# The shared feed-forward in float32r parts, with its weights in a ring of column pairs and its down products turned round

## The reference

```python
gate = jax.nn.silu(jnp.einsum('ech,ehi->eci', xg, rg))
up = jnp.einsum('ech,ehi->eci', xg, ru)
eout = jnp.einsum('eci,eih->ech', gate * up, rd)
...
routed = jnp.zeros_like(xf).at[dispatch.reshape(-1)].add(contrib.reshape(-1, h))
shared = jax.nn.silu(x @ sg) * (x @ su) @ sd
return shared + SCALE * routed.reshape(b, s, h)
```

## Time and profile before

| | |
|---|---|
| median of 3 runs | 1663.79 us (1660.51 to 1671.43) |
| profiled execution, its own time | 1664.96 us |
| its span | 1663.2 us |
| TensorE busy | 1557.2 us (94%) |
| VectorE, ScalarE, GpSimd busy | 870.3, 734.2, 696.3 us |

### The profile page before, as it was taken

One profiled execution on the slowest core, in us unless ns is written; L12 is line 12 of the kernel. 1 busy time (PEld: TensorE's weight loads), 2 busy tenths in 40 slices (PEclk: granted clock), 3 DMA queues, 4 the chain that ended last, 5 costly groups with the idle time before them and its releaser, 6 DMA issues. The chain is left out here.

```text
span 1663.2 us, 20499 instructions
## 1 busy us (share of the span) xinstructions
PE 1557.2 (94%) x7136; PEld 747.0 (45%) x7136; DVE 870.3 (52%) x2297; ACT 734.2 (44%) x998; POOL 696.3 (42%) x516
## 2 busy tenths in 40 slices
PE   5699999989999999898999898999999999999998
PEld 3423333323333333332333233555656577777755
DVE  7578878888677865556765723343422111111141
ACT  4754666765566655475545466233211111111111
POOL 4437999987799998153210121400000200000070
PEclk9659999999999999999998888999999999999999
DMA  3551033233231320344432015100040005243071
GB/s 96 145 154 32 23 83 74 74 93 78 65 84 33 78 46 14 73 118 108 124 74 64 28 34 166 61 0 0 0 152 4 23 0 184 92 157 119 16 129 23
DMA packets 76178, 121.39 MB, mean 73 GB/s; under 512 B 15192, under 2 KB 53537, under 8 KB 73003
## 3 DMA queue, kind: packets, MB, share of 16 engines
q1 hardware_dynamic: 72155, 113.62, 24.5%
q0 software_dynamic: 3072, 6.03, 2.1%
q10 hardware_dynamic: 848, 0.43, 0.1%
HBM read 85.05 MB, written 36.96 MB: 73 GB/s over the span
## 5 line engine op out<-in xcount | busy, mean ns | idle before, releaser
L1145 POOL TENSOR_TENSOR sb_prob<-sb_prob,sb_weight 128x1024 f32<-128x1024 f32 x192 | 448.4, 2371 | 44.6 <-ACT sb_prob L1361 44.1
L1361 ACT ACTIVATE sb_prob<-wide 128x1024 f32<-128x1024 f32 (+3 forms) x384 | 347.1, 916 | 210.7 <-PE wide L1974 107.4
L1969 PE MATMUL wide<-sb_stack_q,sb_stack_k 99*128 99x512 bf16 (+3 forms) x896 | 285.7, 369 | 17.4 <-ACT sb_prob L1361 7.5
L1656 DVE CUSTOM_DVE_ANT_0 sb_junk<-bank,sb_bias 128x512 bf16<-128x512 f32 x339 | 226.7, 687 | 61.4 <-PE bank L1944 56.3
L1405 ACT ACTIVATE sb_sil<-wide 128x320 f32<-128x320 f32 (+1 forms) x128 | 66.2, 517 | 436.0 <-PE wide L2048 436.0
L1944 PE MATMUL bank<-sb_stack_k,sb_stack_q 96*128 96x512 bf16 (+3 forms) x597 | 217.6, 383 | 20.0 <-DVE sb_rowmax L1656 5.4
L2048 PE MATMUL wide<-sb_weight,sb_ffn 128*128 128x512 f32 x512 | 233.2, 599 | 0.0
L1989 PE MATMUL wide<-sb_prob,sb_v_aug 128*17 128x512 f32 (+3 forms) x1792 | 225.3, 569 | 7.7 <-ACT sb_o_raw L1374 6.0
L1783 DVE TENSOR_TENSOR sb_act_s<-sb_sil,wide 128x512 f32<-128x512 f32 x64 | 43.9, 687 | 255.0 <-ACT sb_sil L1405 255.0
L1183 POOL DMA_INDIRECT sb_weight<-slots_out,sb_slot_r x32 | 31.5, 986 | 283.9 <-issue 282.1
L2048 PE MATMUL wide<-sb_xgT,sb_big 128*128 128x320 f32 x512 | 147.0, 433 | 1.4 <-ACT sb_xgT L1420 1.4
(11 more groups left out here) (272 smaller groups left out, 1827.9 us busy)
## 6 DMA issues: line engine op xcount, KB each, us to landing
sb_stack_k<-parts SPq DMA_DIRECT2D x32, 256.0 KB, 6.8
o_raw<-sb_o_raw SPq DMA_DIRECT2D x32, 256.0 KB, 2.3
sb_big<-rg SPq DMA_DIRECT2D x8, 1024.0 KB, 4.9
sb_big<-ru SPq DMA_DIRECT2D x8, 1024.0 KB, 7.3
sb_big<-rd SPq DMA_DIRECT2D x8, 1024.0 KB, 10.6
sb_stack_q<-parts SPq DMA_DIRECT2D x16, 384.0 KB, 5.1
parts<-sb_o_norm SPq DMA_DIRECT2D x40, 128.0 KB
sb_stack_q<-parts SPq DMA_DIRECT2D x16, 256.0 KB, 5.6
```

The costliest lines, as they stand in the source:

```text
L1145: e.tensor_tensor(p, p, weight_of(*u[1:]), ALU.mult).then_inc(weigh_p.handle, 1)
L1361: e.activation(p[:, :, first:HALF], sc[:, :, first:HALF], ACT.Exp).then_inc(SC.empty_sem(u), 1)
L1656: e.tensor_tensor_reduce(out=junk[:, i % 2, 0:hi - lo], in0=BK.tile(u)[:, 0:hi - lo], in1=bias[:, qt, lo:hi], scale=1.0, scalar=-3e38, op0 ...
L1969: i = e.matmul(sc[:, j * HALF + first:(j + 1) * HALF], stack_k[0:ROWS_M, n % 3, g, kt * P:(kt + 1) * P], stack_q[0:ROWS_M, n % 3, g, half ...
```

## The change

The shared feed-forward is computed from parts. ScalarE copies the weights of a pair of columns (1536 elements a partition), and the tokens of a chunk, to float32r (the high part); GpSimd or VectorE subtracts that from the original (the low part). Gate and up are three products each of high by high, high by low and low by high, with float32r operands. The activation is split in the same way ("act"), and the down products are turned round: weights are the stationary side, 512 tokens the moving one, so the accumulator holds features as rows; VectorE adds it to xT ("total_T") and TensorE transposes the sum back ("yT").

All weights, shared and expert, now come through a ring of five buffers by pairs of columns ("wload", three transfers of 256 KB), the shared ones anew for each chunk. High and low parts have three buffers each. Pairs of chunks 0 and 1, and the first three of chunk 3, get their low part from GpSimd, the others from VectorE. The downs come two columns behind their gate and up (LAG). The sends are spread over steps. An expert's products stay true float32. New and changed functions, cut:

```diff
...
 COLUMNS_S, COLUMNS_R = I_S // P, I_R // P
 CHUNKS = T // HALF
 TPC = HALF // P
+COLUMNS = [("s", tc, i) for tc in range(CHUNKS - 1) for i in range(COLUMNS_S)]
+COLUMNS += [("e", x, i) for x in range(E) for i in range(COLUMNS_R)]
+COLUMNS += [("s", CHUNKS - 1, i) for i in range(COLUMNS_S)]
+N_PAIRS, EARLY, AHEAD_SPLIT = len(COLUMNS) // 2, 2, 3
+RAWS, HIS = 5, 3
...
+def low_by_pool(p):
+    return column_pair(p)[0][1] < CHUNKS // 2 or p in LAST_CHUNK[:AHEAD_SPLIT]
...
+def sends(b):
+    return [("send", b, t) for t in range(b * NT, (b + 1) * NT)]
...
+def columns_of_chunk(plan, kind, x, others, late):
+    n = COLUMNS_S if kind == "s" else COLUMNS_R
+    for i in range(n):
+        k = COLUMNS.index((kind, x, i))
+        plan.append(("gu", kind, x, i))
+        if kind == "s":
+            plan.append(("act", kind, x, i))
+        p = k // 2 + 1
+        if k % 2 == 0 and p in SPLITS and p not in LAST_CHUNK[:AHEAD_SPLIT]:
+            plan += halved(p)
+        if k >= LAG:
+            ended(plan, k - LAG)
+        plan += late.pop(i, [])
         for _ in range(STEPS_PER_COLUMN):
             if others:
                 plan += flat([others.pop(0)])
-    return plan + [("resT", tc), ("down", "s", tc, COLUMNS_S - 1)]
+def halved(p):
+    return [("split", p)] + ([("wload", p + RAWS)] if p + RAWS < N_PAIRS else [])
+def ended(plan, k):
+    of_, x, i = COLUMNS[k]
+    plan.append(("down", of_, x, i))
+    if k % 2 and of_ == "e" and k // 2 + RAWS < N_PAIRS:
+        plan.append(("wload", k // 2 + RAWS))
+    if of_ == "s" and i == COLUMNS_S - 1:
+        plan.append(("total_T", x))
+    if of_ == "e" and i == COLUMNS_R - 1:
+        plan.append(("eout", x))
+def turned(tc):
+    return {LAG + 1: [("yT", tc, 0), ("yT", tc, 1)]}
+FIRST = [("hsplit", 0), ("split", 0)]
...
     last, route = (1, 1, NQ // 2 - 1), route_plan(0)
...
+    others = [("num", *last), *route[:3], ("inv", *last), *route[3:5], ("times", *last), PAUSE]
+    mixer = mix_plan(1)
+    at = mixer.index(("hT", 1, 0, DC - 1))
+    mixer = mixer[:at + 1] + [("hsplit", 2)] + mixer[at + 1:]
+    others += beside(sends(0), [outputs(1, 1)[k:k + NH] for k in (0, NH)] + mixer)
+    plan = [("wload", RAWS)]
+    columns_of_chunk(plan, "s", 0, others, {COLUMNS_S - 4: [("hsplit", 1)]})
+    columns_of_chunk(plan, "s", 1, others, turned(0))
+    plan += flat(others) + [("pad",)]
+    columns_of_chunk(plan, "s", 2, route_plan(1) + sends(1), turned(1))
+    plan.append(("fetch", 0))
     for x in range(E):
...
+        late = turned(2) if x == 0 else {}
+        if x + 1 < E:
+            late[3] = late.get(3, []) + [("fetch", x + 1)]
+        if x == 2:
+            late[4] = [("hsplit", 3)]
+        if x == E - 1:
+            for k in range(AHEAD_SPLIT):
+                late[2 * k + 3] = late.get(2 * k + 3, []) + halved(LAST_CHUNK[k])
+        columns_of_chunk(plan, "e", x, [], late)
     last = B * NT - TPC
...
+    others = [PAUSE] * 4 + [("gather", t) for t in range(AHEAD)] + [PAUSE] * 2
     for t in range(B * NT):
         others += [[("combine", t), ("gather", t + AHEAD)] if t + AHEAD < B * NT else ("combine", t)]
-    plan += shared_plan(CHUNKS - 1, others) + flat(others)
+    columns_of_chunk(plan, "s", CHUNKS - 1, others, {})
+    plan += flat(others)
+    for k in range(LAG):
+        ended(plan, len(COLUMNS) - LAG + k)
+    plan += [("yT", CHUNKS - 1, 0), ("yT", CHUNKS - 1, 1)]
     return plan + [("total", t) for t in range(last, B * NT, 2)]
...
+            def load_pair(p):
+                kind, x, i = column_pair(p)[0]
+                g, u, d = ([A["sg"], A["su"], A["sd"]] if kind == "s" else [A["rg"][x], A["ru"][x], A["rd"][x]])
+                if p >= RAWS:
+                    was = p - RAWS
+                    w.wait_ge(low_done(("split", was)) if is_shared(was) else down_done(*column_pair(was)[1]))
...
+            for p in range(EARLY, RAWS):
+                load_pair(p)
             for u in TAIL:
                 kind = u[0]
...
+                if kind == "wload":
+                    load_pair(u[1])
                 elif kind in ("num", "inv"):
                     division(u)
                 elif kind == "fetch":
                     x = u[1]
                     for b in range(B):
                         w.wait_ge(sent[b].end)
+                    for mark in mixer_done:
+                        w.wait_ge(mark)
                     if x >= 2:
...
+            def low(u):
+                w.wait_ge(high_a.after(u))
...
+                if u[0] == "split":
+                    high, of_, to = w_hi(u[1]), w_raw(u[1]), w_lo(u[1])
+                else:
+                    cols = slice(u[1] * HALF, (u[1] + 1) * HALF)
+                    high, of_, to = h_part(u[1], 0), hT[:, :, cols], h_part(u[1], 1)
+                e.tensor_tensor(to.bitcast(F32R), of_, high, ALU.subtract).then_inc(low_p.handle, 1)
...
+            def high(u):
+                if u[0] == "split":
+                    p = u[1]
+                    k = SPLITS.index(p)
+                    w.wait_ge(w_in[p % RAWS].after((p, 2)))
+                    if k >= HIS:
+                        w.wait_ge(down_done(*column_pair(SPLITS[k - HIS])[1]))
+                    to, of_ = w_hi(p), w_raw(p)
+                else:
+                    tc = u[1]
...
+                    for v in hT_of(tc):
+                        w.wait_ge(ring(v).emptied(v))
...
+                    to, of_ = h_part(tc, 0), hT[:, :, tc * HALF:(tc + 1) * HALF]
+                e.activation(to.bitcast(F32R), of_, ACT.Copy).then_inc(high_a.handle, 1)
+            for u in FIRST:
+                high(u)
...
+                    if i >= ACTS:
+                        w.wait_ge(down_done(*GUS[i - ACTS][1:]))
+                    e.activation(act_slot(*u[1:])[0][:, 0:n], SC.tile(u)[:, 0:n], ACT.Silu).then_inc(silu_a.handle, 1)
+                elif kind == "act":
+                    a, a_hi, _ = act_slot(*u[1:])
+                    w.wait_ge(SC.emptied(("gu", *u[1:])))
+                    e.activation(a_hi.bitcast(F32R), a, ACT.Copy).then_inc(act_high.handle, 1)
...
+                    n = HALF if u[1] == "s" else CAP
+                    a = act_slot(*u[1:])[0][:, 0:n]
                     w.wait_ge(silu_a.after(u))
-                    e.tensor_tensor(dst, sil[:, j % 2, 0:n], gu[:, HALF:HALF + n], ALU.mult).then_inc(SC.empty_sem(u), 1)
+                    e.tensor_tensor(a, a, SC.tile(u)[:, HALF:HALF + n], ALU.mult).then_inc(SC.empty_sem(u), 1)
+                elif kind == "act":
+                    a, a_hi, a_lo = act_slot(*u[1:])
+                    w.wait_ge(act_high.after(u))
+                    e.tensor_tensor(a_lo.bitcast(F32R), a, a_hi, ALU.subtract).then_inc(act_low.handle, 1)
+                elif u in low_d.value:
+                    w.wait_ge(high_a.after(u))
+                    e.tensor_tensor(w_lo(u[1]).bitcast(F32R), w_raw(u[1]), w_hi(u[1]), ALU.subtract).then_inc(low_d.handle, 1)
+                elif kind == "total_T":
+                    tc = u[1]
+                    acc = ACC.tile(("acc", "s", tc))[:].rearrange("p (c t) -> p c t", c=DC)
+                    w.wait_ge(acc_done.after(("s", tc)))
+                    for k in range(2):
+                        half = slice(k * HALF // 2, (k + 1) * HALF // 2)
...
+                        e.tensor_tensor(xs, acc[:, :, half], xs, ALU.add).then_inc(
+                            ACC.empty_sem(("acc", "s", tc)) if k else half_T.handle, 1)
...
                     gu = SC.tile(u)
+                    p, j = pair_weights(of_, x, i)
                     if of_ == "s":
...
+                        w.wait_ge(low_done(("hsplit", x)))
+                        w.wait_ge(low_done(("split", p)))
+                        w.wait_ge(SC.vacant(u))
+                        hi, lo = (h_part(x, k).bitcast(F32R) for k in range(2))
+                        for z in range(2):
+                            o = gu[:, z * HALF:(z + 1) * HALF]
+                            for c in range(DC):
+                                w_h, w_l = (gate_up(piece, z, c, j).bitcast(F32R) for piece in (w_hi(p), w_lo(p)))
+                                e.matmul(o, w_h, hi[:, c], start=(c == 0), stop=False)
+                                e.matmul(o, w_h, lo[:, c], start=False, stop=False)
+                                m = e.matmul(o, w_l, hi[:, c], start=False, stop=(c == DC - 1))
                     else:
-                        w.wait_ge(expert_in[x % 2].after((x, 2)))
+                        w.wait_ge(w_in[p % RAWS].after((p, 2)))
                         for c in range(DC):
                             w.wait_ge(BT.emptied(("xT", x, c)))
...
                     m.then_inc(SC.full_sem(u), 1)
                 elif kind == "down":
                     _, of_, x, i = u
                     acc = ACC.tile(("acc", of_, x))
+                    p, j = pair_weights(of_, x, i)
+                    final = i == (COLUMNS_S if of_ == "s" else COLUMNS_R) - 1
```

(23 more changed lines are left out.)

265 lines of the change are left out of this document (119 added, 146 removed).

## The result

The changed kernel takes 1762.82 us (median of 4, 1759.39 to 1765.79) beside 1667.49 us of the kernel before in the same session: a ratio of 1.058, 95% interval 1.0551 to 1.0609. A second session gave 1759.58 us and 1.055 (1.0525 to 1.0575). Two executions of the whole study stand far outside every group (4998.86 us of the kernel before, 3637.83 us of the kernel with five edits) and are left unexplained; the medians hardly notice them. The forecast was 1709 us with a range up to 1745: the sign was right, and the forecast rise (45 us) was half of what came. The profiled execution has a span of 1762.2 us, 99 more than before.

A forecast was written before the change was run, and what follows sets the result against it. The feed-forward tail was taken to be bound by TensorE alone. Savings of 81.7 and 3.3 us against added waits, clock loss and other terms summed to +45 on 1664.96 us, giving 1709 us, range 1666 to 1745.

The forecast's parts named there:

- columns: Shared feed-forward columns: 18 one-pass float32r matmuls of 0.216 us, 3.88 us in place of 5.16, 64 times: -81.7 us.
- What costs nothing: Put at 0: weight reloads per chunk, spread sends, dropped expert padding, third tile's unchanged 256-column stream, downs lagging two columns.
- pairs in chunks 0 and 1: Each of 15 pairs waits about 2.05 us for its split, +31 us; mixer cover and later queues taken to cancel.
- chunk 2 and route: VectorE lows leave 0.2 us a pair; with route products +6 us there and +3 in chunk 0.
- experts' fetch: Next expert's token loads queue on SyncE behind a later pair's load: seven waits of 6.0 us, +38.5 us net.
- clock: Half clock behind TensorE gaps: 2.4 us in each of seven experts, 17, and 7 in chunk 0; +24 us.
- chunk 3: VectorE needs about 5.2 us a column against 3.88, and the end chain is 1.5 us longer: +10 us.
- Rival 3: Shared products: a float32r matmul takes two passes, 430 ns, a column 7.7 us; 1897 us in all; chance 0.07.
- the prediction's sign: For the last shared chunk, what would show the forecast right: chunk 3 nearer 75 than 62 us.
- Rival 2: GpSimd lows and VectorE subtractions obstruct each other, 1.3 us more in each of 18 pairs: +24, 1733 us; chance 0.13.
- Rival 1: One pass and the waits vanish, pairs cost 0, fetches land in 3.0 us: faster, 1626 us; chance 0.10.
- rival 4: Most waits are half as forecast, mixer covers the pairs, fetches cost 5 us: within 1%, 1672 us; chance 0.13.

The follow-up runs named there:

- kernel with five edits: Changed kernel plus 128-column third tile, tokens loaded earlier, splits one column sooner, last division first, and VectorE making the lows of chunks 0 and 1: 1663.01 us, ratio 0.997.

## Why the prediction missed, step by step

The forecast sum was +45, the profile shows +99. Three terms make up the difference: the columns (16 us), a load that was put at nothing (22) and the clock (some 23); the others are off by 5 us or less and cancel. By its own steps:

| step | forecast | measured |
|---|---|---|
| columns | -81.7 | -65.3 (64 x 1.02) |
| residual products and transposes | -3.3 | as forecast (0.12 us a transpose) |
| "What costs nothing": padding | 0 | +22 (64 x 0.34) |
| start | +7.8 | 7.6, with the tail beginning 3.0 us sooner in this execution |
| pairs in chunks 0 and 1 | +31 | 13.8 behind lows, 13.9 behind the mixer |
| chunk 2 and route | +9 | 13.8 |
| last division | +9.8 | 8.9 |
| experts' fetch | +38.5 | 38.5 (42.0 less 3.5) |
| clock | +24 | about 47 (what the other rows leave of 99) |
| chunk 3 | +10 | +6.7 (waits 7.3 after 0; the end 3.7 after 4.3) |

(Two sums of the prediction are off by a little and change nothing: 64 x 1.28 is 81.9, and a chain of 7.4 us against 5.18 leaves 2.2 a pair, 33 us for 15. The kernel before has waits of its own, 1.5 us in chunk 0 and 1.4 before the first expert, that the change takes in.)

*The columns.* One pass was right; the term was mis-sized by 16 us, because 0.23 us was taken to be 0.216. The bf16 spacing came from the nearest row, and 18 products a column multiply a difference of 14 ns by 1152. The Trainium skill, "FP8 and Floating Point Precision", section TensorE Precision Notes, has true float32 as four passes, which fits 0.86 us after 0.23; of the reduced form it gives neither the passes nor a duration, so that one pass is enough is this trace's to say. Rival 3 (two passes) is out.

*What costs nothing.* This is the step that failed in kind: a term put at 0 that measured 22 us. I wrote that the padding "goes, GpSimd's, off the path" and that the third tile "streams the same 256 columns". Both are true, and the stationary side was left out: where 64 columns are loaded between loads of 128, load and matmul no longer overlap, and it costs 0.11 us on the gate-up and 0.23 on the down, 64 times. The experiments with 128 columns gave it back (18 us beside the gaps, 21 without them). The trace of before could not show it, as every load in its tail was 128 wide, but I gave no bound for it either.

*The experts' fetch.* SyncE's order was followed through the queue, and term and place came out as written: seven waits of 5.1 to 6.5 us, released by the token load. The experiment that only reorders the queue removes them.

*The clock.* The mechanism and the size of one gap were right: 2.2 us for each of the seven gaps in the experts (15.7 by the experiment) after 2.4 and 17 forecast. What was wrong was where I looked for gaps: 7 us in chunk 0 and none elsewhere. In the four shared chunks the float32r products alone lost 11.5, 4.6, 6.6 and 4.2 us (the sum, over the timeline, of what their distances have over 0.23 us), 27 us. The other terms leave some 5 us more, which would fall to the slower mixer and routing products between them; that remainder is by subtraction and not measured. The waits that I priced outside the experts were to be priced with the half clock behind them as well.

*The pairs.* "I let the two cancel" held in size (27.7 after 31), which is luck, and not in kind. Waits of 2 us before every second gate-up did not come: there is one of 6.1 us in chunk 0 and five of 0.6 to 3.1 in chunk 1. Half of the sum is the mixer. Its products come after the same number of columns, which now are 1.02 us shorter each, but that is the smaller part: with true float32 columns of 5.15 us the mixer's waits are still 10.5 of 13.9 us (1.3 in the kernel before). The rest must come from the work that the change adds to the queues of the other engines, or from its order; which of it, no run separates.

*Chunk 3* came out smaller than its term, and yet took 86.4 us, not the 75 of the prediction's sign: to 66.2 us of columns come two expert downs by the lag (3.1), the waits (7.3), the lower clock (4.2) and the end (3.7), and the prediction's sign had neither the lag nor the clock. The division came as forecast. Of *chunk 2 and route*, 13.8 after 9, 5.6 us are the stall at 1350, which the prediction does not have, and 8.2 the routing.

*Rival 2* was real, where I did not look. I priced it for lows against VectorE's new subtractions, 1.3 us in each pair; those meet three times in the changed kernel, for 0.4 to 0.6 us each. It struck instructions of the mixer more: 3.2, 3.2 and 2.2 us in the changed kernel, and 3.2 and 3.1 at two scans as soon as the splits came sooner. It also struck GpSimd once (1.3 us). How much of the 99 us that is, no run tells. The Trainium skill, "SBUF — State Buffer", section on the two separate sides, has a GpSimd instruction and a VectorE one with two SBUF inputs exclude each other: the one that starts first holds the shared ports for its whole length, and the other waits. The rows agree with it in both directions: scans of 5.48 and 5.39 us that began inside a low, and a low of 4.76 us that began inside a scan. (The one of 4.53 us is recorded as beginning 0.03 us before the low, and waited.) Rival 1 and rival 4 fell with the fetches.

The range missed by 18 us: its upper end was contention with late fetches, and had no place for the 22 us of a load that no row of before showed, nor for half clock in the shared chunks.

## What to carry to other kernels

Taking work from the engine that bounds a kernel pays only as far as the chains beside it are shorter than the new rhythm: here 65 us of TensorE's work were worth 18, and after four mends of queue orders and load widths the kernel was level with the one before. Go through each stage with the new, shorter unit and ask what else was just hidden by the old one; price each new gap of TensorE of 5 to 6 us with the two us of half clock that followed it here. When a tile changes its width, look at both sides of the matmul, the loaded side too.
